# Causal masks moved: transposed scores masked on GpSimd behind the exponential, plain scores of query blocks 2 and 3 inside VectorE's maximum

## What is computed

```python
attn = jnp.einsum('nhqd,nhkd->nhqk', q, k) * scale
causal = jnp.tril(jnp.ones((t, t), dtype=bool))
attn = jnp.where(causal, attn, -jnp.inf)
attn = jax.nn.softmax(attn, axis=-1)
out = jnp.einsum('nhqk,nhkd->nhqd', attn, v)
```

## Time and profile before

| | us |
|---|---|
| three runs | 759.87, 759.89, 760.43 |
| median | 759.89 |
| span of the profiled execution, first to last instruction | 757.7 |
| TensorE busy | 660.7 (87%) |
| VectorE busy | 514.1 (68%) |
| ScalarE busy | 342.2 (45%) |
| GpSimd busy | 151.8 (20%) |

### The profile page before, as it was taken

How to read it: one execution, slowest core, us unless ns; L and a number is a source line. 1 busy time by engine, 2 the same in 40 slices (tenths; PEclk the granted TensorE clock), 3 DMA queues, 4 the chain that set the end, 5 groups by cost and what they waited for, 6 DMA issues and landing times.

```text
span 757.7 us, 13009 instructions
## 1 busy us (share of the span) xinstructions
PE 660.7 (87%) x5007; PEld 464.5 (61%) x5007; DVE 514.1 (68%) x1313; ACT 342.2 (45%) x472; POOL 151.8 (20%) x145
## 2 busy tenths in 40 slices
PE   1478889999989899999999998999989899998664
PEld 0333556565655699898998785775555655555443
DVE  6578776777743536658537467777786778666993
ACT  1110566656575444433444432335546455674221
POOL 5301010100011010010021301302203010345764
PEclk9995999999999999999999999999999999999985
DMA  5405876454320000000000200211211211000000
GB/s 152 126 22 147 173 218 132 85 141 75 66 55 14 1 1 1 1 1 1 1 1 1 63 1 12 75 23 28 83 42 27 65 45 35 25 12 1 14 15 28
DMA packets 29325, 38.07 MB, mean 50 GB/s; under 512 B 3719, under 2 KB 23185, under 8 KB 29265
## 3 DMA queue, kind: packets, MB, share of 16 engines
q1 hardware_dynamic: 29265, 37.25, 20.3%
HBM read 26.33 MB, written 10.88 MB: 49 GB/s over the span
## 4 chain that ended last, share of the span: by engine, by line
PE 64%; DVE 25%; issue 5%; ACT 3%; POOL 1%; DMA 0%; POOLq 0%; DVEq 0%; ACTq 0%
PE ps L989 14%; PE ps L486 9%; PE ps L444 7%; DVE mx L663 6%; PE ps L465 6%; PE ps L979 4%; PE ps L512 3%; PE ps L981 3%; PE ps L980 3%; DVE xn L926 3%; PE ps L447 2%; ACT pT L557 1%; PE ps L494 1%; PE ps L469 1%; DVE x L1063 1%
## 5 line engine op out<-in xcount | busy, mean ns | idle before, releaser
L663 DVE TENSOR_REDUCE mx<-ps 128x1 f32<-128x384 f32 (+3 forms) x352 | 215.5, 637 | 72.5 <-PE ps L447 70.4
L557 ACT ACTIVATE pT<-ps 128x1024 f32<-128x1024 f32 x160 | 162.1, 1023 | 86.9 <-PE ps L469 71.9
L1024 ACT ACTIVATE pT<-ps,b1c 128x512 f32<-128x512 f32 x128 | 87.8, 687 | 129.6 <-PE ps L981 128.7
L989 PEld LDWEIGHTS ps<-w_sb,pT 128*128 128x128 f32 x1024 | 132.2, 191 | 11.8 <-issue 1.3
L989 PE MATMUL ps<-w_sb,pT 128*128 128x128 f32 x1024 | 135.5, 275 | 0.0
L447 PE MATMUL ps<-mask_qk,identb 128*128 128x128 bf16 (+2 forms) x352 | 90.2, 256 | 0.0
L444 PE MATMUL ps<-stA 96*128 96x128 bf16 (+3 forms) x256 | 69.6, 332 | 19.2 <-DVE mx L663 14.3
L486 PE MATMUL ps<-pT,vA 128*32 128x512 f32 (+3 forms) x1024 | 77.9, 439 | 0.7 <-ACT pT L557 0.7
L1063 DVE SCALAR_TENSOR_TENSOR x<-ps,comb,x 128x128 f32<-128x128 f32 x128 | 36.0, 344 | 58.4 <-PE ps L989 58.3
L444 PE MATMUL ps<-kA,stA 96*128 96x128 bf16 (+3 forms) x256 | 63.7, 304 | 12.8 <-DVE mx L663 11.6
L979 PE MATMUL ps<-x_hi,w_hi 128*128 128x512 f32 x128 | 62.9, 491 | 1.2 <-DVE w_lo L1045 1.0
(11 more groups left out here) (232 smaller groups left out, 964.1 us busy)
## 6 DMA issues: line engine op xcount, KB each, us to landing
stA<-stack_scratch SPq DMA_DIRECT2D x48, 192.0 KB, 3.4
stB<-stack_scratch SPq DMA_DIRECT2D x48, 192.0 KB, 4.5
stack_scratch<-part SPq DMA_DIRECT2D x12, 384.0 KB, 3.2
w_sb<-in_L_ffn_W_dram SPq DMA_DIRECT2D x16, 256.0 KB, 5.6
stack_scratch<-part SPq DMA_DIRECT2D x12, 256.0 KB, 3.1
stack_scratch<-part SPq DMA_DIRECT2D x12, 128.0 KB, 3.1
x<-in_L_attn_z_dram SPq DMA_DIRECT2D x4, 256.0 KB, 4.4
out_dram<-x SPq DMA_DIRECT2D x4, 256.0 KB, 2.3
```

The lines of the kernel that those rows point to most:

```text
L557: act.activation(dst_, src, ACT.Exp, scale=SCALE).then_inc(a["ex"], 1)
L663: nc.vector.tensor_reduce(mx[:, g % 2, qb, heads[0]:heads[0] + nh], ps[:, S_BANK[n % 2], 0:nh * w].rearrange("p (h k) -> p h k", h=nh), AX ...
L989: last = pe.matmul(ps[:, ST_BANK[1] + m % 2, f * P:(f + 1) * P], hT[:, (m % 2) * FC + c, f * P:(f + 1) * P], w2_sb[:, e, c, :], start=(c = ...
L1024: act.activation(hT[:, (m % 2) * FC + f, :], ps[:, ST_BANK[0] + n % 2, :], ACT.Gelu, bias=b1c[:, e * FC + f:e * FC + f + 1]).then_inc(M["g ...
```

## The change

Three things are done, in both layers.

1. Plain scores of blocks 2 and 3 (S3 to S10, 8 of 11 units): the mask product is gone. VectorE takes one tensor_tensor_reduce, which adds mask_row (bfloat16, 128 x 512, zero but for its last 128 columns) to the unit, writes the sum back to the same PSUM bank and gives the maximum. It is built as two instructions, the sum and the read of the accumulator. S0 to S2 are as before.
2. Transposed scores: all mask products are gone. The exponential is taken of unmasked scores, and GpSimd sets the part of pT behind the diagonal to zero with affine_select: two instructions for each of the units 0 to 3 (256 and 128 columns), one for unit 4 (512 columns). PV waits for the new semaphore cut, which the last of them raises, in place of ex.
3. VectorE waits once, behind its first two fills, until mask_row is made. mask_kq is gone, mask_row takes its place among the set-up work of GpSimd.

```diff
@@ attention_tensor, S
-                    pe.matmul(ps[:, bank, m * w:(m + 1) * w], stA[:, 0, h, qb * P:w], kk[:, 0:w],
-                              start=(m == 0), stop=False)
+                    last = pe.matmul(ps[:, bank, m * w:(m + 1) * w], stA[:, 0, h, qb * P:w], kk[:, 0:w],
+                                     start=(m == 0), stop=(qb >= 2))
+                if qb >= 2:
+                    last.then_inc(a["sc"], 1)
+                    return
@@ attention_tensor, ST
-                if u < HG:
-                    pe.matmul(ps[:, base, 0:P], identb[:], mask_kq[:], start=False, stop=True)
-                    last = pe.matmul(ps[:, base + 1, :].rearrange("p (a c) -> p a c", a=NB)[:, 0:4:3, :], identb[:],
-                                     mask_kq[:].unsqueeze(1).broadcast_to([P, 2, P]), start=False, stop=True)
-                else:
-                    for c in range(2):
-                        last = pe.matmul(ps[:, base + c, :].rearrange("p (h k) -> p h k", h=2)[:, :, 0:P], identb[:],
-                                         mask_kq[:].unsqueeze(1).broadcast_to([P, 2, P]), start=False, stop=True)
                 last.then_inc(a["st"], 1)
             elif name == "PV":
-                pe.wait_ge(a["ex"], (i + 1) * NV)
+                pe.wait_ge(a["cut"], i + 1)
@@ attention_vector, S
+                if qb >= 2:
+
+                    nc.vector.tensor_tensor_reduce(
+                        ps[:, S_BANK[n % 2], 0:w], ps[:, S_BANK[n % 2], 0:w], mask_row[:, T - w:T], 1.0, LOWEST, ALU.add, ALU.max,
+                        mx[:, g % 2, qb, heads[0]:heads[0] + 1]).then_inc(a["maxd"], 1)
+                    return
@@ attention_gpsimd
+        def below_diagonal(blocks, n):
+
+            return nc.gpsimd.affine_select(blocks, blocks, compare_op=ALU.is_ge, fill=0.0, base=0,
+                                           pattern=[[0, n], [1, P]], channel_multiplier=-1)
+
+            elif name == "ST":
+
+                pool.wait_ge(a["ex"], i * NV + u + 1)
+                if u < HG:
+                    two_ = pT[:, g % 2, u, 0:1024].rearrange("p (a c) -> p a c", a=2)[:, :, 0:P]
+                    below_diagonal(two_, 2)
+                    below_diagonal(pT[:, g % 2, u:u + 1, KB_AT[3][0]:KB_AT[3][0] + P], 1)
+                else:
+                    below_diagonal(pT[:, g % 2, :, KB_AT[2][0]:KB_AT[2][0] + P], HG).then_inc(a["cut"], 1)
@@ the start of VectorE's instructions
             nc.vector.memset(ones[:], 1.0).then_inc(made_w, 1)
+            dve.wait_ge(made, 3)
```

More of the change, by code:

```diff
@@ L55 @@
 NEG = -1e30
+LOWEST = -3e38
 EPS_LN = 1e-5
@@ L256, in network @@
         mask_qk = sb("mask_qk", [P, P], BF16)
-        mask_kq = sb("mask_kq", [P, P], BF16)
+        mask_row = sb("mask_row", [P, T], BF16)
         ones = sb("ones", [P, P])
@@ L374, in network @@
         both = ("xnT q k v qhi khi qrest krest qmid kmid split vraw va store "
-                "sc maxd mt negm mpart mstore st ex pv oTs ot on ont onTs wo xdone").split()
+                "sc maxd mt negm mpart mstore st ex cut pv oTs ot on ont onTs wo xdone").split()
         rotary = "qs ks qf kf qsum ksum kacc kparts rotq rotk bias".split()
@@ L464, in attention_tensor @@
                     kk = stB[:, 1, h, :] if layer == 0 else kA[:, b, :]
-                    pe.matmul(o, kk[:, kb * P:(kb + 1) * P], stB[:, 0, h, kb * P:T], start=(at % 512 == 0), stop=False)
-                if u < HG:
-                    pe.matmul(ps[:, base, 0:P], identb[:], mask_kq[:], start=False, stop=True)
-                    last = pe.matmul(ps[:, base + 1, :].rearrange("p (a c) -> p a c", a=NB)[:, 0:4:3, :], identb[:],
-                                     mask_kq[:].unsqueeze(1).broadcast_to([P, 2, P]), start=False, stop=True)
-                else:
-                    for c in range(2):
-                        last = pe.matmul(ps[:, base + c, :].rearrange("p (h k) -> p h k", h=2)[:, :, 0:P], identb[:],
-                                         mask_kq[:].unsqueeze(1).broadcast_to([P, 2, P]), start=False, stop=True)
+                    last = pe.matmul(o, kk[:, kb * P:(kb + 1) * P], stB[:, 0, h, kb * P:T], start=(at % 512 == 0),
+                                     stop=(kb in (0, 3) or at % 512 > 0))
                 last.then_inc(a["st"], 1)
             elif name == "PV":
-                pe.wait_ge(a["ex"], (i + 1) * NV)
+                pe.wait_ge(a["cut"], i + 1)
                 if i == 0 and layer == 0:
@@ L1390, in _ @@
             nc.gpsimd.tensor_copy(identb[:], ident[:]).then_inc(made, 1)
-            for m, step, mul in ((mask_qk, -1, 1), (mask_kq, 1, -1)):
+            for m, step, mul in ((mask_qk, -1, 1),):
                 link(nc.gpsimd, nc.gpsimd.memset(m[:], 0.0))
@@ L1394, in _ @@
                                         pattern=[[step, P]], channel_multiplier=mul).then_inc(made, 1)
+            link(nc.gpsimd, nc.gpsimd.memset(mask_row[:], 0.0))
+            nc.gpsimd.affine_select(mask_row[:, T - P:T], mask_row[:, T - P:T], compare_op=ALU.is_ge, fill=NEG, base=0,
+                                    pattern=[[-1, P]], channel_multiplier=1).then_inc(made, 1)
             nc.gpsimd.memset(half[:], -0.5).then_inc(made, 1)
```

## The result

The changed kernel takes 768.96 us (median of four runs, 767.42 to 769.86), against 760.16 for the kernel before; the ratio is 1.0102, 95% interval 1.0082 to 1.0121. The predicted time was 756.5: the sign is wrong, while the time lies inside the stated range of 748 to 771, at the end that had been kept for rival 1. One execution of e9 (1048 us) and one of the kernel before (874 us) ran in a much slower state of the chip and count in no ratio. The profiled execution has a span of 768.1 us, 10.4 more than before.

A forecast was written before the change was run, and what follows sets the result against it. TensorE and VectorE alternate, with VectorE nearly as tight as TensorE. Span 757.7 - 6.6 (masks less sums) + 1.6 (end of layer 1) + 0.6 (end of layer 0) + 1.0 (port) = 754.3; with 2.2 outside, 756.5 us; range 748 to 771.

The forecast's parts named there:

- rival 1: S4 to S10, behind PV: VectorE becomes the bound through dearer sums; slower, 771.6 us of span at d = 0.19; chance 0.33.
- The gain from TensorE's masks: TensorE without mask products: 16.7 us before the price of the sums, plus 2.4 and 1.8 at the layers' ends.
- the 21 full groups: Groups with S and ST together, 11 in layer 0 and 10 in layer 1: 12.8 us gained, less 97 d.
- the groups of S alone: Groups without ST: 2.0 us gained in layer 0, less 35 d, and 1.9 in layer 1, less 12 d.
- The price of the sums: VectorE pays d on 144 of the 256 units; at d = 0.07 the gain of 16.7 falls to 6.6 us.
- d: Extra VectorE time per long unit for the sum over a plain reduce: 0.07 us, between 0.04 and 0.19.
- The sign that I named: VectorE's long units of 512 columns starting 0.68 to 0.73 us apart mean the forecast, 0.74 or more rival 1.
- Rival 4: VectorE's sums: reading and writing one PSUM bank halves their rate, some 100 us slower; chance 0.03.
- The port: MP, NORM and the kA steps on VectorE delayed more often by GpSimd steps: +1.0 us, between nothing and 2.5.
- The end of layer 1: Last PV waits for selects behind the second QH on GpSimd: +4.0 us, less 2.4 for masks, so +1.6.
- The end of layer 0: PV waits for selects behind L1142: +1.7 us; two more groups 0.35 each; masks give 1.8; in all +0.6.
- Rival 3: TensorE's clock falls behind its gaps, up to 1 us each; five such places make 761.5 us; chance 0.12.

The follow-up runs named there:

- e9: The changed kernel without the selects: transposed scores not masked at all, PV waits for the exponentials, sums stay; 752.2 us, 0.9891 of the kernel before.
- e14: Kernel before, with GpSimd's selects for transposed scores except in each layer's last batch, which TensorE masks; no sums; 755.4 us, 0.9935 of the kernel before.
- e15: As e14, but GpSimd's selects of unit 0 wait until MP is done on VectorE; 751.7 us, 0.9880 of the kernel before.
- e10: The changed kernel without sums and selects, so no mask but on blocks 0 and 1 of the plain scores; 745.5 us, 0.9785 of the kernel before.
- e16: e9 run again for a trace: the changed kernel without the selects, sums stay; 751.9 us, 0.9889 of the kernel before.
- e1: Selects alone: GpSimd masks the transposed scores as in the change, TensorE the plain scores as before, no sums; 766.1 us, 1.0066 of the kernel before.
- e4: The changed kernel with two GpSimd steps (routing's power, second QH) put behind the last select of their layer; 764.9 us, 1.0065 of the kernel before.
- e5: The changed kernel with a plain maximum instead of the sums, blocks 2 and 3 of the plain scores left unmasked; 760.6 us, 1.0001 of the kernel before.
- e6: The changed kernel with 12 filling products on TensorE ahead of the last PV of each layer; 767.7 us, 1.0075 of the kernel before.
- e13: The changed kernel, but GpSimd's selects of unit 0 wait until MP is done on VectorE; 766.0 us, 1.0072 of the kernel before.

## Why the prediction was wrong, step by step

The ledger compares four profiled executions. Each number is the change of a stretch's length against the kernel before (by the starts of MP); each column has the edits of the one ahead of it and one more. Single executions differ by up to 2 us in a stretch (at the fourth MP, ahead of all selects, e14 is 2.1 us behind e15): by the columns the selects cost 18.5 us, by the medians 16.1.

| stretch | masks gone (e10) | + sums (e16) | + selects (the change) |
|---|---|---|---|
| to the last MP of layer 0 | -6.7 | -3.3 | -0.6 |
| to the first MP of layer 1 | +2.6 | +1.1 | +4.1 |
| to the last MP of layer 1 | -7.2 | -4.1 | -0.2 |
| to the end | -1.7 | -1.8 | +7.2 |
| sum | -13.0 | -8.1 | +10.4 |

- **The gain from TensorE's masks: right in the full groups, too large elsewhere.** In all 20.9 us were counted (16.7, 2.4 and 1.8); e10 measures 16.3. 12.8 were counted over the 21 full groups; in e10's trace they gain 7.2 in layer 0 and 5.3 in layer 1, 12.5. Up to the fifth MP of layer 1 it gains 1.9, as set for the groups of S alone. Those of layer 0 gained nothing where 2.0 was expected (0.5 us behind at the fifth MP). TensorE's scores of 512 columns there last 0.63 us, at the lower clock, with and without masks in most of the stretch; in some executions, with masks (before, e1) and without them (e16), there are shorter stretches at the full clock. What decides that was not settled.
- **The price of the sums: right in size.** 144 d with d = 0.07 is 10.1 us; measured are 7.7 and 8.0, so d is 0.055, between the bounds 0.04 and 0.19. The sign that I named had a wrong base: I read long units 0.65 us apart against the 0.64 of the earlier trace rows as d = 0.01, where a plain reduce without a wait has 0.60. The rest under PV stayed (1.77 us), and of the short rests one of 0.43 is left. Rival 1 forecast a slower kernel, but its cause is refuted: with the sums and without the selects (e9) the kernel is 8.3 us faster than before. That 769.0 lies inside the stated range is therefore luck, since that end of it stood for rival 1. Rival 4 is refuted too (the sum of 512 columns lasts 0.71 us).
- **The port: right in kind, too small.** +1.0 was set, 2.5 at most, on the ground that selects meet MP by chance. They meet it in half of the groups: in 16 of the 32 groups of the kernel before the exponential of ST(0) ends within 0.14 us of the start of MP, which could have been read from its trace. L674, MP's first step, was long there in five groups, and not once, as I had read the earlier trace rows: 0.71, 0.53 twice and 0.20 twice, each time beside a GpSimd step. The four steps of MP last 30.7 us in the changed kernel and 27.4 in e16, and keeping the selects off MP gave back 0.9 to 4.2 us: about 3.
- **The bodies of the layers: more than MP's steps.** By the ledger the selects cost 2.6 and 3.9 us there. Group by group, most of it, 4.5 us, stands in four groups (1.0 to 1.4 each, at 125, 555, 603 and 651 us) in which the changed kernel's trace shows the lower clock; e16's shows it in two of the four. The others lose 0.4 at most. Whether the selects bring these falls stays open.
- **The end of layer 1: mechanism right, size wrong.** The last PV waits for QH's three steps and seven selects, as predicted:

```profile
692.49 1.38 POOL L820 TENSOR_TENSOR w_sb<-w_sb,qs 128x704 f32<-128x704 f32 x1
693.83 2.46 POOL L703 TENSOR_SCALAR_AFFINE_SELECT pT<-pT 128x256 f32<-128x256 f32 x7
```

  (GpSimd in the changed kernel.) The last exponential had ended at 692.71, so this is 3.6 us late, near the 4.0. Left out were the two PVs before it, which stand behind QX and the first QH (they add 1.0 and 1.2 us to the distance from e16), and the lower clock at PV and behind it, 2.1 us at PV alone. In all 9.0 in place of 4.0; the masks of that stretch gave 1.7 to 1.8 (e10, e16) where 2.4 was set.
- **The end of layer 0: too small.** PV goes at 248.35; the routing's power (L1159) and five selects hold it:

```profile
244.85 1.64 POOL L1159 TENSOR_TENSOR two<-two,phalf 128x8 f32<-128x8 f32 x1 [3.23 <-DVE two L1134]
246.44 1.85 POOL L703 TENSOR_SCALAR_AFFINE_SELECT pT<-pT 128x256 f32<-128x256 f32 x5
```

  That is 2.7 us behind its place before, where +1.7 was set, and the PV itself takes 3.81 us on the chain in place of 2.40. The 1.0 more comes with L1159, which starts 1.2 us later than its counterpart before: the routing's own small steps on VectorE, for which it waits, start 0.4 us later and take 0.8 us more, those that lie beside selects. The longest of them (VectorE's timeline, then GpSimd's; before, L1097, it took 0.18):

```profile
239.14 0.63 DVE L1114 TENSOR_SCALAR r<-r 128x32 f32<-128x32 f32 x1
```

```profile
239.10 0.63 POOL L703 TENSOR_SCALAR_AFFINE_SELECT pT<-pT 128x512 f32<-128x512 f32 x1 [0.26 <-ACT pT L554]
```

  So the port also delayed the routing, for which the forecast had set nothing. The 1.8 us of masks gave nothing: in e10 this stretch is 2.6 slower than before without any select, with a granted clock of 0.50 from 220 to 230 us. In the traces without selects in the whole last batch it is 0.7 us shorter to 2.6 longer than before, in those with them (the change, e1, e4, e5, e6, e13) 3.9 to 5.0 longer. So the selects cost some 3 us here (3.0 between the change and e16, 1.8 between e5 and e10), and the spread of the rest goes with the clock of single executions.
- **Rival 3** (the clock) was a price of 1 us a place for five places. It is there, and it matters. At the ends it is a consequence: 1.4 and 2.1 us at the two PVs that GpSimd delays (e6). It should have been part of the forecast's terms there, since the earlier trace rows had shown it: a gap of TensorE, and behind it a stretch half of which ran at the lower level. In the bodies its part is open: the mean granted clock of the changed kernel is 0.947 over its four executions, that of the kernel before 0.963 to 0.965 in the four rounds of experiments.

The step that failed is therefore the price of the selects: 4.0 + 1.7 + 0.7 at the ends and 1.0 for the port, 7.4 us, became 16 (by the ledger 9.0 and 3.0 at the ends and 6.5 in the bodies). With 16 in its place the forecast's own other terms (16.7 and 4.2 for the masks, -10.1 for the sums) would have given a loss of 5. The masks make up the rest: those of the layers' ends and of the first groups were set at 6 us, and 1.7 to 1.8 was found.

## What to carry to other kernels

Work moved to an idle engine still stands in that engine's queue: look at each place where its input comes with that of a neighbouring stage, and at the short VectorE steps (two inputs from SBUF, casts, scalar operations) that lie beside it on the critical chain. Price a new wait on TensorE with its length and with the slower products behind it. And keep such a move where it is hidden: with the masks of the last batch left on TensorE and one wait that keeps GpSimd off MP, half of this change wins about 1% (0.8 and 1.2% in two measurements).

## What was not expected of the hardware

- A maximum that is built as a sum with accumulator costs about 0.055 us a unit over a plain reduce (7.7 and 8.0 us over the 144 units that count), although the 0.14 us read of the accumulator lies beside the next instruction in the timeline.
- One select of 256 columns of float32 in place takes 0.414 us, of 512 columns 0.635; beside it a VectorE step of 16 columns with two SBUF inputs goes from 0.175 to as much as 0.416 us (0.555 in e5), and one step of the routing, 128 x 32, from 0.18 to 0.63.
- At the start of each trace (up to 44 us in e1, up to 84 us in the changed kernel) the granted clock reads 1.00 while scores of 512 columns last 0.63 us, as at the lower level, in place of 0.38: there the durations are to be trusted, not the clock's row.
